# Four chained image layers on one core: gate logits as one product, squares of the next input moved behind the key copies, token transposes moved ahead of a point-wise half

## The chip, the cores and the metric

The kernel runs on one core of one Trainium2 chip. The metric is the device time of one execution in microseconds; lower is better. TensorE is called PE, its weight loads PEld, VectorE DVE, ScalarE ACT, GpSimd POOL and SyncE SP.

## The reference, cut to what matters

Thirty-two images of 256 channels by 28 by 28 pass through four layers, each with a group norm before it and the input added after it.

```python
def reference(x, ...):
    x = x + L0(_gn(x), gate_w, gate_b, expert_w)   # sparsemax gate over 8 experts, mixed 1x1 convolution
    x = x + L1(_gn(x), dw_w, ..., pw_w, ...)       # depthwise 3x3, bn, relu, prune, pointwise 1x1, bn, relu, prune
    x = x + L2(_gn(x), Wqkv, bqkv, Wln, bln)       # linear attention with squared, normalised queries and keys
    x = x + L3(_gn(x), 0)                          # 3x3 box average
    return x

# the gate of L0
pooled = x.mean(axis=(2, 3))
g = sparsemax(pooled @ gate_w.T + gate_b)
w_eff = jnp.einsum('bk,koi->boi', g, expert_w)
out = jnp.einsum('boi,bihw->bohw', w_eff, xs)
```

## The kernel before

**Pipeline.** The 256 channels lie as two halves (j = 0, 1) of 128 partitions. Every engine runs the same function `step(t)` for t from -1 to 36, with t = 8 to 29 in a hardware loop of two steps a turn. In step t seven images are in work, each at another stage: Z = t+1 (input loaded, squares and rounded copy made), A = t (gate and mixed convolution), B = t-1 (depthwise taps), C_ = t-2 (relu and point-wise convolution), D = t-3 (queries and keys), E = t-4 (attention output), F = t-5 (box average). A stage whose image is outside 0 to 31 is left out, so steps 0 to 3 fill the pipeline, steps 4 to 31 are full, and from t = 32 on A is missing (t = 33: A and B; t = 34: A, B and C_). Nothing reorders the work: each engine goes through its `step` as written, and waits on semaphores counted per image.

**PE's order in a step.** `value_out` half 0, `key_norms` (L554), `attention_weights` (L566, L568), `gate_logits` (L509: two products into `small_ps`, one for each half of channels), `value_out` half 1, `attention_out` (L518), `mix_experts` (L648, waits for the gate to be finished), `keys` (L596, L599: seven tiles of 112 tokens in four groups; the fourth group waits for the first two key squares, because it takes their bank), `queries` (L518), `x2_to_tokens` for groups 0 to 2 (L532), `pointwise` (L518), `query_sums` (L618), `x2_to_tokens` group 3, `mixed_conv` (L663), `query_scales` (L630), `keys_x` (L676), `key_sums` (L545), `group_means` (L502). In the steps with C_ but without A, the second half of `pointwise` stands behind `query_sums` and ahead of `x2_to_tokens` group 3.

**DVE's order.** `key_rows` (L968), group norm statistics (L793 to L813), `gate_logits` (L821, L823: the weights of both halves times the pooled input, one instruction on 16 columns), `q_low` (L960), `attention_weights_low` (L981, waits for ACT), `sparsemax` (L831 to L858), `x2_low` (L988), `make_x3` (L922), `h_mask` (L876, waits for ACT), row sums, `h_low`, `mixed_low` (L902), taps (L869), `reciprocal_sums` (L994, waits for the seventh key square), taps, `q_scales` (L1005 to L1011, waits for ACT's L1368), `make_x2` (L890, L894), `make_x1` (L912), `scale_q` (L1019), taps, `kx_low` (L1024).

**ACT's order.** `deviations` (L1161, waits for DVE's L799), `normalise_x2` (L1173), `attention_weights_high` (L1276), relu of h, `x2_high`, `normalise_x3`, `sum_over_h` (L1308), `h_high` (L1317), `scaled_mix` (L1209), `first_tap` (L1292), then the seven squares of keys `square_k` (L1345) with the two squares of the next input `x0_squares` (L1218) behind the second and the third of them, squares of x3, `square_q`, `copy_tokens` (L1246: the transposed tokens scaled into `xT`), fourth powers, `relu_y` 0 (L1335), `sum_over_y` 0 (L1327), `q_norms` (L1368), `relu_y` 1, `sum_over_y` 1, the last token tile, `fourth_powers` (L1268, L1270), `x0_high` (L1227), the squares of x2 and x1, `kx_high` (L1374), `q_high` (L1237), `key_rows` (L1254). Where A is missing, token tiles 0 to 2 are copied before `relu_y` 0, tiles 3 to 5 behind `q_norms`, and tile 6 behind `sum_over_y` 1.

**POOL** scales x1 into `xpad` (L1521); in steps without D and E that waits for the gate product, `gate_step.at(A, 3)`. It also issues the accumulating output DMAs (L1551). **SP** issues the input loads and the output stores.

Of the kernel before, what the change touches and what calls it, by code (L numbers as in the profile page):

```python
# [29 lines left out]
GATE_STEPS = 13  # L30
# [91 lines left out]
def build(nc, x, gate_wT, gate_b, expert_rows, mix_pattern, dw_w, channel_params, pw_wT, w_qk, b_qk, w_vT, w_ln, group_mean, ident, out):  # L122
    with ExitStack() as ctx:
# [88 lines left out]
        gate_in = sb("gate_in", [P, J, EXPERTS])  # L212
        z = sb("z", [P, EXPERTS])
# [233 lines left out]
        def _(pe):  # L447
# [38 lines left out]
            def group_means(Z, A, C_, D, E):  # L486


                if D.active and not A.active:
                    pe.wait_ge(q_root.sem, q_root.at(D))  # L490
                if A.active:
                    pe.wait_ge(gate_step.sem, gate_step.at(A, 4))
                elif A.started:
                    pe.wait_ge(gn_read.sem, gn_read.at(A))
                if Z.active:
                    pe.wait_ge(gn_sums[0].sem, gn_sums[0].at(Z))
                    pe.wait_ge(x0_hi.sem, x0_hi.at(Z))
                for img, layer, made in ((A, 1, x1_ready), (C_, 2, x2_ready), (E, 3, x3_ready)):
                    if img.active:
                        pe.wait_ge(made.sem, made.at(img))  # L500
                        pe.wait_ge(gn_sums[layer].sem, gn_sums[layer].at(img))
                nc.tensor.matmul(small_ps[:, 0:16], gmean[:], gn_in[:].rearrange("p l n -> p (l n)"), start=True,  # L502
                                 stop=True).then_inc(gn_mm.sem, 1)

            def gate_logits(A):
                pe.wait_ge(gn_read.sem, gn_read.at(A))
                pe.wait_ge(gate_step.sem, gate_step.at(A, 3))
                for j in range(J):
                    mm = nc.tensor.matmul(small_ps[:, 0:EXPERTS], ones[:], gate_in[:, j, :], start=(j == 0),  # L509
                                          stop=(j == J - 1))  # L510
                mm.then_inc(gate_mm.sem, 1)
# [168 lines left out]
            def step(t):  # L680
# [29 lines left out]
                if D.active:  # L710
                    query_sums(A, D)
                if C_.active and not A.active:
                    pointwise(C_, range(1, 2))
                if D.active:
                    x2_to_tokens(D, range(3, 4))
# [15 lines left out]
        def _(dve):  # L731
# [84 lines left out]
            def gate_logits(A):  # L816
# [6 lines left out]
                nc.vector.tensor_tensor(gate_in[:], gate_w_sb[:],  # L823
                                        pooled[:, 1, :].unsqueeze(2).to_broadcast([P, J, EXPERTS]),
                                        ALU.mult).then_inc(s.sem, 1)

            def sparsemax(A):
# [4 lines left out]
                dve.wait_ge(s.sem, s.at(A, 4))  # L832
# [3 lines left out]
                dve.wait_ge(s.sem, s.at(A, 5))  # L836
                nc.vector.tensor_tensor(zz[:, 1], zz[:, 0], z[:].unsqueeze(1).to_broadcast([P, EXPERTS, EXPERTS]),
                                        ALU.mult).then_inc(s.sem, 1)
                dve.wait_ge(s.sem, s.at(A, 6))
                nc.vector.tensor_reduce(upper[:, 0:2, :], zz[:], AX.X, ALU.add).then_inc(s.sem, 1)  # L840
                dve.wait_ge(s.sem, s.at(A, 7))
                nc.vector.reciprocal(upper[:, 2, :], upper[:, 0, :]).then_inc(s.sem, 1)
                dve.wait_ge(s.sem, s.at(A, 8))
                nc.vector.scalar_tensor_tensor(upper[:, 3, :], upper[:, 1, :], 1.0, upper[:, 2, :], ALU.subtract,
                                               ALU.mult).then_inc(s.sem, 1)
                dve.wait_ge(s.sem, s.at(A, 9))
                nc.vector.tensor_reduce(tau[:], upper[:, 3, :], AX.X, ALU.max).then_inc(s.sem, 1)
                dve.wait_ge(s.sem, s.at(A, 10))
                nc.vector.scalar_tensor_tensor(gate[:], z[:], tau[:], mix_const[:, 0:EXPERTS], ALU.subtract,
                                               ALU.mult).then_inc(s.sem, 1)  # L850
                dve.wait_ge(s.sem, s.at(A, 11))
                nc.vector.tensor_reduce(gate_own[:], gate[:].rearrange("p (g k) -> p g k", g=PACKED), AX.X,
                                        ALU.add).then_inc(s.sem, 1)
                dve.wait_ge(s.sem, s.at(A, 12))
# [251 lines left out]
        def _(act):  # L1106
# [270 lines left out]
            def step(t):  # L1377
# [42 lines left out]
                for m in range(M):  # L1420
                    if D.active:
                        square_k(D, m)
                    if Z.active and 0 < m <= J:
                        x0_squares(Z, m - 1)
# [20 lines left out]
                if D.active:  # L1445
                    q_norms(A, D)
                    if not A.active:
                        copy_tokens(D, range(3, 6))
# [5 lines left out]
                if D.active:  # L1454
                    copy_tokens(D, range(6, M))
# [22 lines left out]
        def _(pool):  # L1478
# [27 lines left out]
            def normalise_x1(A, B, C_, D, E):  # L1506
# [7 lines left out]
                elif A.active:  # L1514
                    pool.wait_ge(gate_step.sem, gate_step.at(A, 3))
# [117 lines left out]
```

## Time and profile before

| | us |
|---|---|
| median of 3 runs (lowest, highest) | 1503.64 (1500.41, 1505.68) |
| profiled execution, its own time | 1500.17 |
| its span | 1498.5 |
| PE / PEld busy | 1406.2 (94%) / 1238.0 (83%) |
| DVE busy | 1346.3 (90%) |
| ACT busy | 1283.9 (86%) |
| POOL busy | 322.8 (22%) |
| HBM over the span | 85 GB/s |

The span goes from the first to the last instruction; the profiled execution's time is 1.7 us above it. Shares of busy time are means over the filling steps, the full steps and the emptying steps, which have different limits, so the rows below are of one stage each. A timeline row gives start, length, engine, line, operation and the number of instructions merged; an idle time in brackets is that of the engine before the row, with what ended it.

### The profile page before, as it was taken

Reading aid. Unit: us, or ns where it says so; the run is one execution under the profiler, and the core shown is the slowest. Engines: PE = TensorE matmul, PEld = TensorE weight load, DVE = VectorE, ACT = ScalarE, POOL = GpSimd, SP = SyncE. Lnnn points to the kernel's source line nnn. Section 1 sums busy time; section 2 is a strip of 40 time slices with the busy share of each in tenths; the row PEclk is TensorE's granted clock in tenths of the full one; section 3 lists DMA queues with packets and bytes.
Section 4 is the critical chain, followed back from the end, with each engine's and each line's share of the span. In section 5 each row is a group of like instructions: output and inputs, shape, how many; then the busy total and the mean of one; then the engine's idle time right before and its main releaser. Section 6 shows DMA issues by size and latency. Waiting matters only on the chain. (4 is left out here: it accounts for less than half of the span.)

```text
span 1498.5 us, 28620 instructions
## 1 busy us (share of the span) xinstructions
PE 1406.2 (94%) x9538; PEld 1238.0 (83%) x9538; DVE 1346.3 (90%) x2337; ACT 1283.9 (86%) x2624; POOL 322.8 (22%) x298
## 2 busy tenths in 40 slices
PE   3469999999999999999999999999999999999994
PEld 2358898988889898888988888888898888988883
DVE  4889899999999999999999999999999999998647
ACT  5478989989889999988989998898999989888862
POOL 4111122222222221222222122222212222211100
PEclk9679999999999999999999999999999999999997
DMA  4001054353444534344453444345444434444342
GB/s 161 22 22 44 23 108 100 74 108 87 88 89 102 107 70 102 87 94 98 86 107 87 85 94 96 89 86 107 91 80 102 90 86 86 87 88 84 67 66 65
DMA packets 45574, 127.91 MB, mean 85 GB/s; under 512 B 3793, under 2 KB 4817, under 8 KB 45522
## 3 DMA queue, kind: packets, MB, share of 16 engines
q0 software_dynamic: 24480, 72.26, 29.4%
q1 hardware_dynamic: 20946, 54.99, 10.4%
q8 instruction: 29, 0.48, 0.1%
q14 instruction: 23, 0.19, 0.0%
q10 hardware_dynamic: 96, 0.00, 0.0%
HBM read 29.29 MB, written 97.94 MB: 85 GB/s over the span
## 5 line engine op out<-in xcount | busy, mean ns | idle before, releaser
L869 DVE SCALAR_TENSOR_TENSOR h<-xpad,dw_sb,h 128x784 f32<-128x784 f32 x512 | 498.8, 1041 | 0.0
L676 PE MATMUL tile_ps<-k,xT 112*128 112x256 f32 x896 | 200.9, 382 | 3.3 <-ACT xT L1246 3.3
L599 PE MATMUL tile_ps<-wqk,xn_parts 128*112 128x256 f32 x1344 | 191.8, 295 | 0.0
L1551 POOL DMA_DIRECT2D out<-row_sums x90 | 108.8, 1209 | 379.9 <-DMA out<-row_sums 214.7
L676 PEld LDWEIGHTS tile_ps<-k,xT 112*128 112x128 f32 x896 | 168.9, 191 | 25.6 <-issue 3.6
L1538 POOL TENSOR_TENSOR x_parts<-x,x_parts 128x784 fp32r<-128x784 f32 x64 | 109.5, 1729 | 335.5 <-ACT x_parts L1227 335.5
L1167 ACT ACTIVATE junk<-x 128x784 bf16<-128x784 f32 x192 | 163.4, 860 | 9.2 <-DVE x L922 6.4
L599 PEld LDWEIGHTS tile_ps<-wqk,xn_parts 128*112 128x112 f32 x1344 | 170.4, 176 | 0.2
L518 PE MATMUL conv_ps<-xn_parts,w_out 128*128 128x392 f32 x768 | 153.4, 348 | 0.0
L518 PE MATMUL conv_ps<-hq_parts,attn_parts 128*128 128x392 f32 x768 | 145.2, 344 | 3.0 <-DVE attn_parts L981 0.9
L663 PE MATMUL conv_ps<-x_parts,mixed_parts 128*128 128x392 f32 (+1 forms) x768 | 145.3, 345 | 2.1 <-DVE mixed_parts L902 2.1
L518 PE MATMUL conv_ps<-hq_parts,pw_parts 128*128 128x392 f32 x768 | 145.0, 343 | 2.2 <-DVE hq_parts L882 2.2
L518 PEld LDWEIGHTS conv_ps<-hq_parts,attn_parts 128*128 128x128 f32 x768 | 135.0, 188 | 13.0 <-DVE attn_parts L981 13.0
L518 PE MATMUL conv_ps<-xn_parts,wqk 128*128 128x392 f32 x768 | 142.1, 340 | 0.0
L663 PEld LDWEIGHTS conv_ps<-x_parts,mixed_parts 128*128 128x128 f32 x768 | 135.8, 189 | 3.9 <-issue 3.8
L518 PEld LDWEIGHTS conv_ps<-hq_parts,pw_parts 128*128 128x128 f32 x768 | 134.6, 188 | 4.5 <-DVE hq_parts L882 3.9
L518 PEld LDWEIGHTS conv_ps<-xn_parts,wqk 128*128 128x128 f32 x768 | 135.5, 188 | 0.0
L518 PEld LDWEIGHTS conv_ps<-xn_parts,w_out 128*128 128x128 f32 x768 | 134.8, 189 | 0.0
L1521 POOL TENSOR_SCALAR xpad<-x,gn_rs 128x784 f32<-128x784 f32 x64 | 63.6, 1003 | 201.7 <-DVE xn_parts L988 166.5
L1246 ACT ACTIVATE xT<-tile_ps,k_rec 112x256 f32<-112x256 f32 x224 | 89.5, 523 | 0.0
L1345 ACT ACTIVATE k<-tile_ps 112x256 f32<-112x256 f32 x224 | 83.1, 390 | 4.3 <-PE tile_ps L599 4.2
L648 PE MATMUL small_ps<-expert_sb,mix_w 128*32 128x512 f32 x512 | 68.4, 656 | 10.6 <-DVE mix_w L858 10.6
(161 smaller groups left out, 2741.3 us busy)
## 6 DMA issues: line engine op xcount, KB each, us to landing
out<-row_sums POOLq DMA_DIRECT2D x90, 784.0 KB, 7.1
x<-x SPq DMA_DIRECT2D x32, 784.0 KB, 4.3
out<-x SPq DMA_DIRECT2D x30, 784.0 KB, 3.4
expert_sb<-expert_rows SPq DMA_DIRECT2D x8, 256.0 KB, 5.2
out<-x SPq DMA_DIRECT2D x4, 392.0 KB, 2.3
x<-w_qk SPq DMA_DIRECT2D x1, 512.0 KB, 3.6
x<-w_vT SPq DMA_DIRECT2D x1, 256.0 KB, 7.8
x<-w_ln SPq DMA_DIRECT2D x1, 256.0 KB, 7.6
```

The source lines that it names most:

```text
L518: mm = nc.tensor.matmul(conv_ps[:, 2 * j + a, 0:HALF], wt[:, half(j)], act[:, a * HALF:(a + 1) * HALF], start=(first and i == 0), stop=(la ...
L599: mm = nc.tensor.matmul(dst, xn2_parts[:, u, i, m * TOK:(m + 1) * TOK], wqk[:, v, i, C:2 * C], start=False, stop=(i == J - 1 and u == 1))
L648: mm = nc.tensor.matmul(small_ps[s * SUB:(s + 1) * SUB, :], mix_w[:, g, :], expert_sb[:, g, s, :], start=(g == 0), stop=(g == PACKED - 1), ...
L663: mm = nc.tensor.matmul(conv_ps[:, 2 * j + a, 0:width], mixed_parts[:, u, i * C + j * P:i * C + (j + 1) * P], x0_parts[:, v, i, a * HALF:a ...
L676: mm = nc.tensor.matmul(tile_ps[:, KX_BANK, i * C:(i + 1) * C], xT[:, m, half(i)], k2[:, m, :], start=(m == 0), stop=(m == M - 1))
L869: nc.vector.scalar_tensor_tensor(acc, view, scalar, acc, ALU.mult, ALU.add).then_inc(dw_step[j].sem, 1)
L1167: nc.scalar.activation(junk[:, j * HW:(j + 1) * HW], source[:, j, :], ACT.Square, accum_out=gn_in[:, layer, 2 + j:3 + j]).then_inc(gn_sums ...
L1246: nc.scalar.activation(xT[:, m, :], tile_ps[0:TOK, XT_BANK[m // 2], m % 2 * C:(m % 2 + 1) * C], ACT.Identity, scale=k_rec[:, m:m + 1]).the ...
L1345: nc.scalar.activation(k2[:, m, :], tile_ps[0:TOK, K_BANK[m // 2], m % 2 * C:(m % 2 + 1) * C], ACT.Square, accum_out=k_sum[:, m:m + 1]).th ...
L1521: nc.gpsimd.tensor_scalar(xpad[:, j, 1:1 + H, 1:1 + W], x1[:, B.odd, j, :].rearrange("p (h w) -> p h w", w=W), gn_r[:, 1, j:j + 1], gn_s[: ...
L1538: nc.gpsimd.tensor_tensor(x0_parts[:, 1, j, 0:HW], x0[:, Z.odd, j, :], x0_parts[:, 0, j, 0:HW].bitcast(F32), ALU.subtract).then_inc(x0_lo. ...
L1551: pool.dma_start(out_dram[F.times(1)], rows, accum_op=ALU.add).then_inc(rows_added[n].of(F), 16)
```

## The change

Three edits. (1) The gate: DVE multiplies the weights of half 0 by the pooled column into `gate_half`, waits for that, and multiplies half 1 and adds `gate_half` in a second instruction, `gate_sum`; PE forms the logits from `gate_sum` in one product in place of two. All later counts of `gate_step` go up by one; POOL's wait in steps without D and E too. (2) ACT does the seven `square_k` first and the two `x0_squares` behind them. (3) In steps with C_ and D but without A, PE does `x2_to_tokens` group 3 ahead of the second half of `pointwise`, and ACT copies token tiles 3 to 6 in one go behind `q_norms`.

```diff
@@ PE
             def gate_logits(A):
                 pe.wait_ge(gn_read.sem, gn_read.at(A))
-                pe.wait_ge(gate_step.sem, gate_step.at(A, 3))
-                for j in range(J):
-                    mm = nc.tensor.matmul(small_ps[:, 0:EXPERTS], ones[:], gate_in[:, j, :], start=(j == 0),
-                                          stop=(j == J - 1))
-                mm.then_inc(gate_mm.sem, 1)
+                pe.wait_ge(gate_step.sem, gate_step.at(A, 4))
+                nc.tensor.matmul(small_ps[:, 0:EXPERTS], ones[:], gate_sum, start=True, stop=True).then_inc(gate_mm.sem, 1)
...
                 if D.active:
                     query_sums(A, D)
+                if D.active:
+                    x2_to_tokens(D, range(3, 4))
                 if C_.active and not A.active:
                     pointwise(C_, range(1, 2))
-                if D.active:
-                    x2_to_tokens(D, range(3, 4))
@@ DVE
-                nc.vector.tensor_tensor(gate_in[:], gate_w_sb[:],
-                                        pooled[:, 1, :].unsqueeze(2).to_broadcast([P, J, EXPERTS]),
-                                        ALU.mult).then_inc(s.sem, 1)
+                nc.vector.tensor_scalar(gate_half, gate_w_sb[:, 0, :], pooled[:, 1, 0:1], None, ALU.mult).then_inc(s.sem, 1)
+                dve.wait_ge(s.sem, s.at(A, 3))
+                nc.vector.scalar_tensor_tensor(gate_sum, gate_w_sb[:, 1, :], pooled[:, 1, 1:2], gate_half, ALU.mult,
+                                               ALU.add).then_inc(s.sem, 1)
@@ ACT
-                for m in range(M):
-                    if D.active:
+                if D.active:
+                    for m in range(M):
                         square_k(D, m)
-                    if Z.active and 0 < m <= J:
-                        x0_squares(Z, m - 1)
+                if Z.active:
+                    for j in range(J):
+                        x0_squares(Z, j)
...
                 if D.active:
                     q_norms(A, D)
                     if not A.active:
-                        copy_tokens(D, range(3, 6))
+                        copy_tokens(D, range(3, M))
...
                 if D.active:
-                    copy_tokens(D, range(6, M))
+                    if A.active:
+                        copy_tokens(D, range(6, M))
                     fourth_powers(D)
@@ POOL
                 elif A.active:
-                    pool.wait_ge(gate_step.sem, gate_step.at(A, 3))
+                    pool.wait_ge(gate_step.sem, gate_step.at(A, 4))
```

## Rows read from the trace of the kernel before

**Rows 1.** Page: busy time of each engine, share of the span, instructions.

```profile
PE 1406.2 (94%) x9538; PEld 1238.0 (83%) x9538; DVE 1346.3 (90%) x2337; ACT 1283.9 (86%) x2624; POOL 322.8 (22%) x298
```

**Rows 2.** Busy time by stretch (columns named in the first line): steps 4 to 31, and step 33.

```profile
core 0: us, PE busy (x) PEld busy (x) DVE busy (x) ACT busy (x) POOL busy (x), PEclk, DMA share, GB/s
...
130.60:1347.10 1216.50, 1210.71 (x8319) 1070.43 (x8317) 1147.00 (x1988) 1104.97 (x2259) 273.21 (x246) 1.00 0.43 89
...
1387.20:1429.10 41.90, 38.34 (x256) 34.86 (x254) 24.46 (x41) 32.91 (x65) 4.40 (x4) 0.96 0.40 77
```

**Rows 3.** Who waited for whom in steps 4 to 31: total us, times, longest.

```profile
ACT gn_sd L1161 <- DVE gn_var L799: 55.9, 28, 2.0
...
PEld conv_ps L518 <- DVE attn_parts L981: 11.2, 28, 0.5
DVE k_eps L994 <- ACT k L1345: 9.7, 27, 2.8
PEld tile_ps L596 <- ACT k L1345: 9.6, 27, 0.4
...
DVE q_alpha L1005 <- ACT q_norm L1368: 8.9, 27, 0.4
```

**Rows 4.** Timeline of weight loads around the gate product, step 20.

```profile
829.96 0.53 PEld L509 LDWEIGHTS small_ps<-gate_in,ones 128*128 128x128 f32 x4
830.41 0.84 PEld L518 LDWEIGHTS conv_ps<-xn_parts,w_out 128*128 128x128 f32 x5
```

**Rows 5.** Timeline of step 20: ACT's start of the step, then DVE.

```profile
828.55 0.21 ACT L1161 ACTIVATE gn_sd<-gn_var 128x8 f32<-128x8 f32 x1 [2.02 <-DVE gn_var L799]
...
829.32 0.16 DVE L821 TENSOR_TENSOR pooled<-pooled,gn_rs 128x2 f32<-128x2 f32 x1
829.52 0.19 DVE L823 TENSOR_TENSOR gate_in<-gate_w_sb,pooled 128x16 f32<-128x16 f32 x1
...
831.95 0.88 DVE L981 SCALAR_TENSOR_TENSOR attn_parts<-tile_ps,k_inv,attn_parts 128x256 fp32r<-128x256 f32 x2 [0.16 <-ACT attn_parts L1276]
...
839.33 0.17 DVE L876 TENSOR_SCALAR hmask<-h_over 128x2 f32<-128x2 f32 x1 [0.49 <-ACT over L1308]
...
857.21 1.38 DVE L1005 RECIPROCAL q_alpha<-q_norm 128x196 f32<-128x196 f32 x1 [0.32 <-ACT q_norm L1368]
```

**Rows 6.** Timeline: the gate in step 0; ACT in step 2.

```profile
12.63 0.17 DVE L823 TENSOR_TENSOR gate_in<-gate_w_sb,pooled 128x16 f32<-128x16 f32 x1
12.95 0.99 PE L509 MATMUL small_ps<-gate_in,ones 128*128 128x8 f32 x4 [3.42 <-DVE gate_in L823]
...
64.14 2.04 ACT L1292 ACTIVATE h<-xpad,dw_sb 128x784 f32<-128x784 f32 x2 [0.29 <-POOL xpad L1521]
```

**Rows 7.** Timeline: ACT's squares and PE's fourth group of keys, step 20.

```profile
843.98 0.38 ACT L1345 ACTIVATE k<-tile_ps 112x256 f32<-112x256 f32 x1
...
844.34 0.86 ACT L1218 ACTIVATE junk<-x 128x784 bf16<-128x784 f32 x1
...
844.57 0.96 PE L599 MATMUL tile_ps<-wqk,xn_parts 128*112 128x256 f32 x6
```

**Rows 8.** Timeline of PE in step 20, where nothing holds up L676.

```profile
860.70 0.59 PE L630 MATMUL tile_ps<-kx_parts,picks 128*128 128x196 f32 x4
861.12 6.22 PE L676 MATMUL tile_ps<-k,xT 112*128 112x256 f32 x28
```

**Rows 9.** Timeline of PE, end of step 32 to end of step 33.

```profile
1391.58 0.38 PE L554 MATMUL tile_ps<-norm_weight,k_rows 128*128 128x2 f32 x2 [1.70 <-DVE k_rows L968]
...
1418.65 0.69 PE L630 MATMUL tile_ps<-kx_parts,picks 128*128 128x196 f32 x4 [0.19 <-DVE kx_parts L1011]
1421.01 6.28 PE L676 MATMUL tile_ps<-k,xT 112*128 112x256 f32 x28 [1.66 <-ACT xT L1246]
```

**Rows 10.** Timeline of ACT in step 32.

```profile
1378.59 0.45 ACT L1246 ACTIVATE xT<-tile_ps,k_rec 112x256 f32<-112x256 f32 x1
1378.95 0.19 ACT L1268 ACTIVATE k_rec<-k_rec 112x7 f32<-112x7 f32 x1
```

More of the change, by code:

```diff
@@ L29 @@
 PACKED = EXPERTS // STRIPS
-GATE_STEPS = 13
+GATE_STEPS = 14
 XW = HW + 2
@@ L212, in build @@
         gate_in = sb("gate_in", [P, J, EXPERTS])
+        gate_half, gate_sum = gate_in[:, 0, :], gate_in[:, 1, :]
         z = sb("z", [P, EXPERTS])
@@ L491, in group_means @@
                 if A.active:
-                    pe.wait_ge(gate_step.sem, gate_step.at(A, 4))
+                    pe.wait_ge(gate_step.sem, gate_step.at(A, 5))
                 elif A.started:
@@ L831, in sparsemax @@
                 nc.vector.tensor_tensor(z[:], small_ps[:, 0:EXPERTS], gate_b_sb[:], ALU.add).then_inc(s.sem, 1)
-                dve.wait_ge(s.sem, s.at(A, 4))
+                dve.wait_ge(s.sem, s.at(A, 5))
                 nc.vector.tensor_tensor(zz[:, 0], z[:].unsqueeze(1).to_broadcast([P, EXPERTS, EXPERTS]),
@@ L835, in sparsemax @@
                                         ALU.is_ge).then_inc(s.sem, 1)
-                dve.wait_ge(s.sem, s.at(A, 5))
+                dve.wait_ge(s.sem, s.at(A, 6))
                 nc.vector.tensor_tensor(zz[:, 1], zz[:, 0], z[:].unsqueeze(1).to_broadcast([P, EXPERTS, EXPERTS]),
                                         ALU.mult).then_inc(s.sem, 1)
-                dve.wait_ge(s.sem, s.at(A, 6))
+                dve.wait_ge(s.sem, s.at(A, 7))
                 nc.vector.tensor_reduce(upper[:, 0:2, :], zz[:], AX.X, ALU.add).then_inc(s.sem, 1)
-                dve.wait_ge(s.sem, s.at(A, 7))
+                dve.wait_ge(s.sem, s.at(A, 8))
                 nc.vector.reciprocal(upper[:, 2, :], upper[:, 0, :]).then_inc(s.sem, 1)
-                dve.wait_ge(s.sem, s.at(A, 8))
+                dve.wait_ge(s.sem, s.at(A, 9))
                 nc.vector.scalar_tensor_tensor(upper[:, 3, :], upper[:, 1, :], 1.0, upper[:, 2, :], ALU.subtract,
                                                ALU.mult).then_inc(s.sem, 1)
-                dve.wait_ge(s.sem, s.at(A, 9))
+                dve.wait_ge(s.sem, s.at(A, 10))
                 nc.vector.tensor_reduce(tau[:], upper[:, 3, :], AX.X, ALU.max).then_inc(s.sem, 1)
-                dve.wait_ge(s.sem, s.at(A, 10))
+                dve.wait_ge(s.sem, s.at(A, 11))
                 nc.vector.scalar_tensor_tensor(gate[:], z[:], tau[:], mix_const[:, 0:EXPERTS], ALU.subtract,
                                                ALU.mult).then_inc(s.sem, 1)
-                dve.wait_ge(s.sem, s.at(A, 11))
+                dve.wait_ge(s.sem, s.at(A, 12))
                 nc.vector.tensor_reduce(gate_own[:], gate[:].rearrange("p (g k) -> p g k", g=PACKED), AX.X,
                                         ALU.add).then_inc(s.sem, 1)
-                dve.wait_ge(s.sem, s.at(A, 12))
+                dve.wait_ge(s.sem, s.at(A, 13))
                 dve.wait_ge(setup_pool, SETUP_POOL)
```

## The prediction, made before the changed kernel was run

> **What bounds the kernel now.** I read the page first. PE is busy 94%, DVE 90%, ACT 86% [rows 1]; that names no bound, since three engines are nearly full. So I took the busy times by stretch. In steps 4 to 31 PE is busy 1210.71 of 1216.50 us at full clock [rows 2]: 28 steps of 43.45 us, in each of which PE stands still for 5.79 / 28 = 0.21 us. The small rest matters: an engine that is the bound by itself waits for nobody. The view of waits says for whom PE waits: its weight loads wait 9.6 us in all for ACT's key squares at the fourth group of keys, and 11.2 us for DVE's low part of the attention weights [rows 3]. (These are waits of the load queue; the matmuls already in the array hide a good part, which is why the matmuls' idle time is less than their sum.)
>
> Then I followed ACT and DVE round one step. ACT waits for DVE's variance at the start of the step, 55.9 / 28 = 2.0 us; DVE waits for ACT's root of the query sums, 8.9 / 27 = 0.33 us [rows 3]. Between L1161 and L1368 ACT has no wait for PE, and between L1005 and L799 DVE has none, in any full step. So ACT's stretch (L1161 to L1368, 857.21 - 828.55 = 28.7 us in step 20 [rows 5]) and DVE's (L1005 to L799, the other 14.8 us) release each other in a ring, and their sum is the step. **The full steps are set by this ring of ACT and DVE, and PE runs 0.2 us a step ahead of it.** DVE's waits in a full step all lie inside ACT's stretch: 0.16 us at L981 and 0.49 at L876 in step 20 [rows 5], and 9.7 / 27 = 0.36 at L994 and 0.33 at L1005 on the mean [rows 3]. They are the room that DVE has.
>
> Steps 0 to 3 are serial: PE stands idle 3.42 us for the gate in step 0 [rows 6]. In steps 32 and 33 PE waits for the last token tile before L676, 1.66 us each, and between the two 1.70 us before L554 for DVE [rows 9].
>
> **Edit 1, the gate, full steps.** PE drops two of four load and matmul pairs (each product is two). Four take 830.41 - 829.96 = 0.45 us [rows 4], so PE saves 0.225 us a step. DVE gets one more dependent small instruction. Two such follow each other by 829.52 - 829.32 = 0.20 us [rows 5], so DVE pays 0.20 us a step. The sum of halves is then ready at 829.52 + 0.20 + 0.17 = 829.89, and PE's load stood at 829.96 [rows 4, 5]. From ready to matmul takes 0.15 us where PE is waiting (12.80 to 12.95 [rows 6]), so PE is at most 0.1 us late, less than it saves. Behind the added wait on DVE stand the two `q_low` and L981. Of the 0.20 us the wait at L981 takes 0.16 and the wait at L876 the other 0.04, with 0.45 us to spare. As L876 is where DVE next feeds ACT, the ring does not feel it. PE's 0.225 us is in no ring: PE reaches attention_out earlier and waits longer for L981, then for the key squares. Both are worth **0.0 us**. Bounds: -0.225 x 28 = -6.3 us if PE were the bound, +0.20 x 28 = +5.6 us if DVE's room were gone. I take zero because both pools of idle time are there in every full step.
>
> The Trainium skill, VectorE: DVE Perf Modes, section on the TRN2 errata, speaks against this edit: a VectorE instruction on SBUF pays a fixed term of about 150 cycles whatever its size, so halving the columns halves nothing. The trace agrees: 16 columns take 0.19 us and 2 columns 0.16 [rows 5]. By the page's formula for 8 fp32 columns the added instruction is an estimated 0.17 us, 28 of them 4.6 us where the room is gone.
>
> **Edit 1, steps 0 to 3.** Here the four matmuls take 0.99 us [rows 6], against 0.45 from first load to next load in step 20 [rows 4]: PE's clock is at its lower level, and each pair takes about 0.21. Dropping two saves 0.42 us, and DVE adds 0.20: 0.22 us less each in steps 0, 1 and 3, where mix_experts waits for the gate. In step 2 other DVE work stands between, PE's part is hidden, and POOL's `xpad`, for which ACT waits 0.29 us [rows 6], waits for the gate: +0.20. Together 0.20 - 0.66 = **-0.5 us**. Bounds: -0.9 (step 2 gains too) and +0.8 (nothing saved, four times 0.20).
>
> **Edit 2.** The same nine instructions of ACT stand in the same unbroken stretch, so L1368 comes at the same time. A key square takes 844.34 - 843.98 = 0.36 us, a square of the input 0.86 [rows 7]. The seven end 2 x 0.86 = 1.7 us earlier. DVE's wait of 0.36 us at L994 goes; what is late next is L1368, so the same amount appears at L1005. PE waits for the first two squares only, which stay where they were. The seventh square would start at 843.98 + 5 x 0.36 = 845.78; PE, released by the second square, had its fourth group done at 844.57 + 0.96 = 845.53 [rows 7]. Both count from the second square, so ACT gets no new wait, with 0.25 us to spare. The input load, for which the squares wait, has long landed. **0.0 us**; bounds: -0.36 x 28 = -10 us if DVE's wait there were in the ring, +0.25 x 28 = +7 us if PE's fourth group came 0.5 us later than there and ACT waited.
>
> **Edit 3.** It acts in steps 32 and 33 alone; in step 34 C_ is missing, and the order stays. Step 32: PE's two transposes move ahead of the point-wise half (about 0.2 us, and ACT's relu there is not waiting for PE by then). ACT copies the seventh tile, 1378.95 - 1378.59 = 0.36 us [rows 10], ahead of `sum_over_y` 0, so L890, `make_x2`, `scale_q`, eight taps, L1024 and L968, which follow on DVE without a gap, come 0.36 us later. L676 now starts right behind L630. Where nobody waits it starts 0.42 us after it [rows 8], so L676 wins 1.66 us of idle and some 0.3 of overlap, 1.9 in all. But L554 waits for L968, not for that: it starts 0.36 us later, **+0.36 us**, and the 1.9 us turns into wait before it. Step 33 has no taps: L676 is then on the path. It starts at 1418.65 + 0.36 + 0.42 = 1419.43 in place of 1421.01 [rows 8, 9], and what follows moves with it (L545 next waits for the queries that DVE scales, 0.72 us later than before, by my count 0.3 us ahead of need): **-1.6 us** for the end of step 33, the 0.36 included. Bounds for both steps: -2.0 us (nothing on ACT comes later) and +2.1. The latter is the clock: it is granted at 0.96 over step 33 [rows 2], where PE has idled 1.70 us before L554, and that idle becomes about 4 us in one piece. A second such drop would cost at most what the first does, 0.04 x 41.9 = 1.7 us of full-clock work, on top of +0.36.
>
> **Sum.** -0.5 + 0 + 0 - 1.6 = -2.1 us on the profiled execution's 1500.17 (span 1498.5), or 1498.1. That execution lies 3.5 us below the median of the runs, 1503.64, though within their spread of 5.3. Set against the median: **1501.5 us**, 0.14% less.
>
> **Rivals.** *A: PE is the bound after all.* For it: 94% busy, 0.21 us idle a step. Against it: its waits are for ACT and DVE, and these never wait for PE within the ring. It gives -6.3 - 2.1 = 1495.2 us. The Trainium skill, Perfetto Trace Analysis, Identifying the Most-Contended Engine, would judge PE by its weight loads, 83% [rows 1], and so set DVE's 90% first: against A, and for B.
>
> *B: DVE has no room.* Place: between L823 and L876. It decides when the two waits there (0.65 us in step 20) fall below 0.20; the longer DVE stretch then delays ACT's h_high by the added 0.20 in every full step: +5.6 - 2.1 = 1507.1 us, slower than before. Against it: those waits [rows 5].
>
> *C: edit 3 gives nothing.* The idle piece before L554 costs another stretch at the lower clock, or step 33 keeps a wait elsewhere: the tail is 0 to +2.1 us in place of -1.6, so 1503.1 to 1505.2 us.
>
> *D: edit 2 shortens the ring,* since DVE's wait at L994 goes. Against it: L1005 waits for ACT alone. A third of its bound would be 1498 us.
>
> **How the numbers follow.** Forecast 0.68, A 0.09, B 0.07, C 0.12, D 0.04. The range starts from the forecast with the runs' spread (-3.2, +2.0), widened for C above and D below, and leaves out A and B: 1497.0 to 1505.5 us. About 0.3%, 4.5 us, is what a measurement of this kernel can tell from no change, so faster means below 1499.1: A, part of D and the lower edge of the forecast's spread, 0.15. Slower means above 1508.2: B at its upper edge, 0.05. Within 0.3%: 0.80.
>
> **What would show it.** Full steps still 43.4 to 43.5 us; PE idle about 0.4 us in each in place of 0.21; L509 with two loads; DVE's wait at L994 gone and L1005's near 0.6; L876 still waiting for ACT by about 0.3. In step 32 L676 directly behind L630 and a wait near 4 us before L554; in step 33 no wait before L676, and the step about 2 us shorter. Full steps of 43.2 or 43.65 us would make the prediction wrong, towards A or B.

## The result, and the profile after

The changed kernel takes **1511.72 us**, the median of five runs (1508.11 to 1511.92), and the kernel before 1504.6 us in five runs beside it. The ratio is **1.0046, with a 95% interval of 1.0028 to 1.0064**: slower, by about 7 us, where 2.1 us less was forecast and nothing above 1505.5 was in the range. The profiled execution took 1508.11 us, span 1506.4; that of before 1500.17, span 1498.5.

The change did what it says. PE issues 64 products fewer and DVE 32 instructions more than in [rows 1]. The page after, busy time of each engine:

```profile
PE 1405.8 (93%) x9474; PEld 1232.0 (82%) x9474; DVE 1353.5 (90%) x2369; ACT 1289.9 (86%) x2624; POOL 305.2 (20%) x298
```

The shares are those of before. The difference stands in the view by stretch. Columns are the start and end, the length, then busy time and count of PE, PEld, DVE, ACT and POOL, PE's granted clock, the DMA share and GB/s. The three rows are steps 4 to 31, step 32 and step 33:

```profile
130.90:1356.60 1225.70, 1211.69 (x8263) 1065.56 (x8261) 1152.32 (x2016) 1111.10 (x2259) 255.20 (x246) 1.00 0.42 89
1356.60:1394.90 38.30, 36.70 (x255) 33.17 (x253) 30.91 (x48) 34.08 (x67) 6.40 (x6) 1.00 0.41 80
1394.90:1437.10 42.20, 38.02 (x255) 34.67 (x253) 26.68 (x43) 32.73 (x65) 4.40 (x4) 0.96 0.38 72
```

The 28 full steps take 1225.70 us where they took 1216.50 [rows 2]; PE is busy one microsecond more (1211.69 against 1210.71) and stands still 14.0 us in place of 5.8. Step by step, from group means to group means:

| us | start of step 4 | full steps, mean of 28 | step 32 | step 33 | span |
|---|---|---|---|---|---|
| before | 130.63 | 43.445 | 40.16 | 41.82 | 1498.5 |
| after | 130.95 | 43.773 | 38.33 | 42.19 | 1506.4 |

So 28 x 0.328 = +9.2 us in the full steps, +0.3 ahead of them, -1.5 in steps 32 and 33. Together that is +8.0, and the spans differ by 7.9. In this pair of traces the tail did what was forecast; **the loss is 0.33 us in each full step, where the forecast had zero.**

The waits of steps 4 to 31 after (engine and line that waits, on whom: total us, times, longest):

```profile
ACT gn_sd L1160 <- DVE gn_var L797: 60.8, 28, 2.3
DVE q_alpha L1004 <- ACT q_norm L1367: 25.3, 28, 2.2
PEld conv_ps L516 <- DVE attn_parts L980: 19.3, 28, 0.7
DVE hmask L875 <- ACT over L1307: 11.6, 27, 0.5
PE conv_ps L516 <- DVE attn_parts L980: 10.2, 28, 0.4
PEld tile_ps L594 <- ACT k L1344: 9.3, 27, 0.4
```

Against [rows 3]: DVE's wait at the seventh key square is gone, as edit 2 meant. But DVE now waits for the root of the query sums 25.3 / 28 = 0.90 us a step in place of 0.33, which is more than the two waits of before together (0.36 + 0.33), and it waits at `h_mask` as long as ever. DVE did not run out of room at these waits; ACT came later. No row names a new wait of ACT, and this is the puzzle: **ACT's stretch from L1160 to L1367 has grown, though no new wait shows in it.**

To find where, I took the starts of successive rows of the ring that the prediction names and averaged their distances over steps 8 to 29. Three parts of it differ between the kernels; the others agree within 0.02 us:

| us, mean of steps 8 to 29 | `xn` to `attn_parts` (ACT) | first key square to queries (ACT) | queries to the next `over` (ACT) | whole ring |
|---|---|---|---|---|
| before | 1.88 | 5.85 | 6.44 | 43.449 |
| edit 1 alone | 2.04 | 5.86 | 6.45 | 43.640 |
| edit 2 alone | 1.88 | 6.09 | 6.39 | 43.627 |
| after | 2.04 | 6.10 | 6.39 | 43.822 |

There are two places, one for each of the first two edits. (In these 22 steps the kernels differ by 0.37 us; the first and the last full steps differ by less, so that the mean of 28 is 0.33.) The rows behind them come with their experiments.

### The profile page after: what moved, and what is told of

It reads as the page before. It is cut to its first block and busy times, and to the rows that moved or that the text cites. A ratio compares the mean times of both kernels' runs of the same rounds, so it can differ in the third digit from the quotient of the medians.

```text
span 1506.4 us, 28543 instructions
## 1 busy us (share of the span) xinstructions
PE 1405.8 (93%) x9474; PEld 1232.0 (82%) x9474; DVE 1353.5 (90%) x2369; ACT 1289.9 (86%) x2624; POOL 305.2 (20%) x298
## 5 line engine op out<-in xcount | busy, mean ns | idle before, releaser
L1160 ACT ACTIVATE gn_sd<-gn_var 128x8 f32<-128x8 f32 x37 | 7.7, 209 | 89.0 <-DVE gn_var L797 89.0
```

The source lines that it names most:

```text
L1160: nc.scalar.activation(gn_sd[:], gn_var[:], ACT.Sqrt).then_inc(gn_sqrt.sem, 1)
```

## The experiments

Twelve kernels ran. The start of step 4 lies between 130.6 and 133.7 us in the executions profiled, and not in step with the edits: edit 3, which touches no step before 32, had 133.0. It goes with PE's granted clock: over the first 133 us that is 0.83 in the three traces that start step 4 by 131.0 us (before, after, edit 2 alone), and 0.79 to 0.81 in the eleven that start it at 131.8 or later. So spans carry up to 3 us that cannot be put down to an edit, and the kernels are compared by their full steps first, by the ratio of their runs second. The kernel before ran again beside each group of kernels, with medians of 1501.1 to 1504.6 us, so a kernel's time is to be read by its ratio.

### Each edit alone

The first, with edit 1 only: the gate's instructions, its counts, and one product.

```diff
-                nc.vector.tensor_tensor(gate_in[:], gate_w_sb[:],
-                                        pooled[:, 1, :].unsqueeze(2).to_broadcast([P, J, EXPERTS]),
-                                        ALU.mult).then_inc(s.sem, 1)
+                nc.vector.tensor_scalar(gate_half, gate_w_sb[:, 0, :], pooled[:, 1, 0:1], None, ALU.mult).then_inc(s.sem, 1)
+                dve.wait_ge(s.sem, s.at(A, 3))
+                nc.vector.scalar_tensor_tensor(gate_sum, gate_w_sb[:, 1, :], pooled[:, 1, 1:2], gate_half, ALU.mult,
+                                               ALU.add).then_inc(s.sem, 1)
```

> The kernel before with edit 1 alone. Theory T (two handshakes): the gate's second VectorE instruction delays k_inv (L976) by 0.31 us, and ScalarE's first attention-weights instruction (L1276), which had 0.2 us to spare, starts 0.17 us later behind its xn instruction: full steps 43.6 us, 28 x 0.17 = +4 to +5 us. Rival B (VectorE alone has no room, edit 1 explains everything): full steps 43.8 us, +8 to +10 us. Rival U (neither edit alone costs, only together): within 1 us of before.

Measured: 1506.52 us, ratio 1.0036 (1.0023 to 1.0049), full steps 43.603 us, +0.16. Step 20 of the kernel before, ACT's `xn` and `attn_parts`, and DVE from the gate on:

```profile
829.23 1.98 ACT L1173 ACTIVATE xn<-x,gn_rs 128x784 f32<-128x784 f32 x2 [0.26 <-DVE gn_rs L813]
831.11 0.81 ACT L1276 ACTIVATE attn_parts<-tile_ps,k_inv 128x256 fp32r<-128x256 f32 x2
...
829.63 0.97 DVE L960 TENSOR_TENSOR hq_parts<-q,hq_parts 128x784 fp32r<-128x784 f32 x1
...
830.72 0.17 DVE L976 RECIPROCAL k_inv<-k_inv 128x2 f32<-128x2 f32 x1
```

The same of the kernel after:

```profile
834.73 1.98 ACT L1172 ACTIVATE xn<-x,gn_rs 128x784 f32<-128x784 f32 x2 [0.26 <-DVE gn_rs L811]
836.77 0.84 ACT L1275 ACTIVATE attn_parts<-tile_ps,k_inv 128x256 fp32r<-128x256 f32 x2
...
835.02 0.23 DVE L821 TENSOR_SCALAR gate_in<-gate_w_sb,pooled 128x8 f32<-128x8 f32 x1
835.28 0.23 DVE L823 SCALAR_TENSOR_TENSOR gate_in<-gate_w_sb,pooled,gate_in 128x8 f32<-128x8 f32 x1
835.44 0.96 DVE L959 TENSOR_TENSOR hq_parts<-q,hq_parts 128x784 fp32r<-128x784 f32 x1
836.32 0.15 DVE L973 TENSOR_SCALAR k_inv<-k_norm 128x2 f32<-128x2 f32 x1
836.51 0.17 DVE L975 RECIPROCAL k_inv<-k_inv 128x2 f32<-128x2 f32 x1
```

ACT's `attn_parts` (the high part of the attention weights) reads `k_inv`, the reciprocal of the key norms. DVE makes that behind the gate and `q_low` 0. Before, it was complete at 830.72 + 0.17 = 830.89, and ACT came for it at 831.11: 0.22 us to spare. In the kernel after it is complete at 836.68, and ACT starts at 836.77, 2.04 us behind the start of `xn` and no longer 1.88. The wait is there, but ACT loses only 0.16 us by it, and the view puts no idle time beside so short a gap. In the kernel with edit 1 alone `k_inv` is complete at 836.06 + 0.17 = 836.23 and ACT starts at 836.33:

```profile
834.28 1.98 ACT L1172 ACTIVATE xn<-x,gn_rs 128x784 f32<-128x784 f32 x2 [0.26 <-DVE gn_rs L811]
836.33 0.84 ACT L1275 ACTIVATE attn_parts<-tile_ps,k_inv 128x256 fp32r<-128x256 f32 x2
...
836.06 0.17 DVE L975 RECIPROCAL k_inv<-k_inv 128x2 f32<-128x2 f32 x1
```

The next, with edit 2 only:

```diff
-                for m in range(M):
-                    if D.active:
+                if D.active:
+                    for m in range(M):
                         square_k(D, m)
-                    if Z.active and 0 < m <= J:
-                        x0_squares(Z, m - 1)
+                if Z.active:
+                    for j in range(J):
+                        x0_squares(Z, j)
                 if E.active:
                     junk_free((Z, gn_sums[0]))
                     sum_squares(3, E, x3_of(E), x3_ready)
```

> The kernel before with edit 2 alone. Theory T: the squares of x3, which wait for the squares of x0 because both write the scratch tile junk, now follow them directly, and ScalarE stands still for about 0.25 us between the two: full steps 43.6 to 43.7 us, +5 to +7 us. Rival B: no change, ScalarE's work is the same, within 1 us of before. Rival U: within 1 us of before.

Measured: 1505.32 us, ratio 1.0030 (1.0019 to 1.0042), full steps 43.609 us, +0.16. The last three lines of that diff, which the change leaves alone, are the cause. The squares of x0 and those of x3 write their unused output into the same scratch tile, `junk`, and `junk_free` makes the x3 squares wait until those of x0 are done. Step 20 with edit 2 alone, ACT (L1218 squares x0, L1167 squares x3):

```profile
849.71 0.90 ACT L1218 ACTIVATE junk<-x 128x784 bf16<-128x784 f32 x1
850.46 0.24 ACT L1218 ACTIVATION_READ_ACCUMULATOR junk<-x 128x1 f32 x1
...
850.81 0.86 ACT L1167 ACTIVATE junk<-x 128x784 bf16<-128x784 f32 x1
...
851.67 0.84 ACT L1167 ACTIVATE junk<-x 128x784 bf16<-128x784 f32 x1
```

From the second x0 square to the first x3 square it is 1.10 us, where two squares that don't wait for each other follow at 0.86: the wait on the instruction directly ahead costs 0.24 us. It was always there, but four key squares stood between the two, so that it was met long before it was asked for. The same gap can be read in the kernel before at a place that no edit touched: the last square of x2 and the first of x1, where `junk_free` stands between the two:

```profile
863.70 0.84 ACT L1167 ACTIVATE junk<-x 128x784 bf16<-128x784 f32 x1
864.45 0.19 ACT L1167 ACTIVATION_READ_ACCUMULATOR junk<-x 128x1 f32 x1
...
864.75 0.86 ACT L1167 ACTIVATE junk<-x 128x784 bf16<-128x784 f32 x1
```

They start 1.05 us apart, while the two x2 squares ahead of them are 0.84 apart. Of the 0.24 us the ring gets 0.05 back between the queries and the next `over` (table above); what ends that part earlier I haven't found.

The third, with edit 3 only (group 3 of the transposes ahead of the second point-wise half in steps with C_ and D but without A, and `copy_tokens(D, range(3, M))` at once).

> The kernel before with edit 3 alone. All theories: full steps stay 43.45 us, steps 32 and 33 together 1.5 us shorter, with the wait before the key norms (L554) near 4 us and none before L676. -1.5 us in the span; the clock rival of the prediction would give 0 to +2 us.

Measured: 1500.77 us, ratio 0.9995 (0.9986 to 1.0003). Full steps are 43.462 us, as before. Step 32 takes 38.29 us and step 33 42.19, together 80.48 in place of 81.98: -1.5 us. But step 34, which the edit leaves alone, takes 38.09 us in this trace in place of 36.73, at a lower granted clock (0.91 against 0.95, the number behind POOL's; first this trace, then the kernel before):

```profile
1430.42:1468.51 38.09, 35.25 (x232) 31.30 (x230) 16.78 (x28) 21.87 (x47) 4.40 (x4) 0.91 0.44 75
1429.07:1465.80 36.73, 33.89 (x231) 30.20 (x229) 16.80 (x28) 21.84 (x47) 4.40 (x4) 0.95 0.35 56
```

Over steps 32 to 34 almost nothing is left of the gain (118.58 us against 118.72), and the interval of the ratio holds both -1.5 us and nothing.

The parts add up: 0.158 + 0.164 = 0.322 us a full step for edits 1 and 2, and 0.328 measured for both.

### Each cause mended in the kernel after

Edit 2's place first. The first x3 square gets a scratch tile of its own, so it waits for nobody.

```diff
+        junk3 = sb("junk3", [P, HW], BF16)
...
-                    junk_free((Z, gn_sums[0]))
-                    sum_squares(3, E, x3_of(E), x3_ready)
+                    if (E - 1).active:
+                        act.wait_ge(gn_sums[3].sem, gn_sums[3].at(E - 1))
+                    for j, spare in enumerate((junk3[:], junk[:, 0:HW])):
+                        act.wait_ge(x3_ready.sem, x3_ready.at(E, j + 1))
+                        if j:
+                            junk_free((Z, gn_sums[0]))
+                        nc.scalar.activation(spare, x3_of(E)[:, j, :], ACT.Square,
+                                             accum_out=gn_in[:, 3, 2 + j:3 + j]).then_inc(gn_sums[3].sem, 1)
```

> The changed kernel, but the first half of x3's squares goes to a scratch tile of its own and the second half to the part that the first x0 square has long left, so that nothing waits for the instruction right ahead of it. Theory T: the 0.25 us stand between the x0 squares and the x3 squares goes, the delay of L1276 stays: full steps 43.6 us, 5 to 7 us less than the changed kernel. Rival B: no change against the changed kernel, full steps 43.8 us. Rival U: back to the time of before, since one of the two is gone.

Measured: 1506.08 us, ratio to before 1.0036 (1.0022 to 1.0049), full steps 43.592, so 0.18 us less than after. The four squares now stand 0.84 us apart (L1435 is the new line):

```profile
851.11 0.91 ACT L1218 ACTIVATE junk<-x 128x784 bf16<-128x784 f32 x1
...
851.95 0.90 ACT L1218 ACTIVATE junk<-x 128x784 bf16<-128x784 f32 x1
...
852.79 0.90 ACT L1435 ACTIVATE junk<-x 128x784 bf16<-128x784 f32 x1
...
853.63 0.90 ACT L1435 ACTIVATE junk<-x 128x784 bf16<-128x784 f32 x1
```

Then edit 1's place: DVE makes `k_inv` ahead of the gate.

```diff
+                if E.active:
+                    key_norms(E)
                 if A.active:
                     gate_logits(A)
                 if E.active:
                     q_low(E, 0)
-                    key_norms(E)
                     q_low(E, 1)
```

> The changed kernel with VectorE's key_norms (L973, L975) put ahead of the gate, so that k_inv no longer stands behind the gate's second instruction; VectorE does the same instructions as in the changed kernel. Theory T (place): ScalarE's L1275 follows xn without a wait, edit 1's 0.16 us a step go, the 0.16 us of edit 2 stay: full steps 43.61 us, 4 to 5 us less than the changed kernel. Rival B (VectorE has no room): the amount of work is the same, so no change: 43.77 us.

Measured: 1505.86 us, ratio 1.0030 (1.0019 to 1.0041), full steps 43.646, 0.13 us less than after. `xn` to `attn_parts` is 1.88 us again, though DVE is as busy as in the kernel after: what mattered was where the gate stood, not how much of it there was. The 0.04 us by which this full step lies above that of edit 2 alone (43.609) I haven't traced.

Both at once:

> The changed kernel with both mends: the scratch tile split and VectorE's key_norms ahead of the gate. Theory T: both added handshakes are gone, full steps 43.45 to 43.50 us as before, and the 1.5 us of edit 3 remain: between -2 and +1 us against before. If a third cost hides in the change, it stays at +3 us or more.

Measured: 1501.89 us, ratio 0.9992 (0.9982 to 1.0001), full steps 43.455, as before (43.445). **The two places are the whole of the 0.33 us.** What is left is the change as the prediction saw it in the full steps, untouched, and no gain that a ratio can show. In this trace steps 32 and 33 take 81.48 us, only 0.5 less than before; why comes with edit 3 below.

### A double dose

If the wait for `k_inv` is the cause of edit 1's cost, a further instruction ahead of it must be paid in full in every step. On edit 1 alone, a third dependent instruction of the same size behind the two (the counts that follow go up by one):

```diff
+                dve.wait_ge(s.sem, s.at(A, 4))
+                nc.vector.tensor_scalar(gate_half, gate_w_sb[:, 0, :], pooled[:, 1, 0:1], None, ALU.mult).then_inc(s.sem, 1)
```

> Edit 1 alone, with one more dependent small VectorE instruction behind gate_sum that nobody needs (PE and GpSimd wait for gate_sum as before). Theory T: the spare 0.15 us ahead of L1276 are used up by edit 1, so the next instruction is paid in full: 0.20 to 0.26 us a step more than edit 1 alone, full steps 43.80 to 43.86 us, +6 to +7 us on edit 1 alone. A theory in which edit 1 costs through its TensorE side or through code placement gives no more than edit 1 alone, 43.60 us.

Measured: 1515.07 us, ratio 1.0090 (1.0077 to 1.0104), full steps 43.941: +0.34 us over edit 1 alone, all of it between `xn` and `attn_parts` (2.38 us). That is more than expected. Averaged over steps 8 to 29 the third instruction costs 0.25 us; the other 0.07 lie ahead of the gate, where `pooled` (L819) starts up to 0.36 us later in some of the steps. What holds it up there isn't known. Now the wait is long enough for the view of waits to name it:

```profile
ACT attn_parts L1277 <- DVE k_inv L977: 9.4, 26, 0.7
```

### Is the ring the bound, and what is PE's saving worth?

A rival to the ring is that PE bounds the step. The kernel before, with the first two key squares moved ahead of ACT's first tap, so that PE's fourth group of keys never waits:

```diff
+                if D.active:
+                    for m in range(2):
+                        square_k(D, m)
                 if B.active and t.number not in (1, 2):
                     for j in range(J):
                         first_tap(B, j)
```

(and the later loop starts at m = 2).

> The kernel before with one move: ScalarE does the first two key squares ahead of first_tap, so that TensorE's fourth group of keys no longer waits. Ring theory: TensorE's wait there (0.17 us in even steps) goes, but the ring is untouched: full steps stay 43.45 us, within 1 us of before. If TensorE were the bound: full steps 43.3 us, -3 to -4 us.

Measured: 1500.0 us, ratio 0.9980 (0.9970 to 0.9989). The full steps are 43.454, unchanged, and the wait at L596 is gone. PE idles 0.15 us a step in place of 0.20: the 0.06 at L518 are as before, and 0.10 at L554 are new. The gain in the traces lies in steps 32 to 34, 115.86 us in place of 118.72, at a granted clock of 0.97 in both; what makes it isn't known. A wait of PE taken away gives nothing while the ring is as long as it was.

Next the ring itself. The squares of x0 leave ACT's stretch between L1161 and L1368 for the time behind it, in which ACT waits for DVE anyway (55.9 us in [rows 3]). On the kernel after with `key_norms` first:

```diff
+                late_x0 = t.number is None or t.number >= 3
...
-                if Z.active:
+                if Z.active and not late_x0:
                     for j in range(J):
                         x0_squares(Z, j)
                 if E.active:
-                    junk_free((Z, gn_sums[0]))
                     sum_squares(3, E, x3_of(E), x3_ready)
...
                     x0_high(Z)
+                    if late_x0:
+                        junk_free((E, gn_sums[3]))
+                        for j in range(J):
+                            x0_squares(Z, j)
...
-                    junk_free((E, gn_sums[3]), (Z, gn_sums[0]))
+                    junk_free((Z, gn_sums[0]), (E, gn_sums[3]))
```

> The changed kernel with key_norms ahead of the gate and, from step 3 on, the two squares of x0 behind x0_high, that is out of ScalarE's stretch of the ring and into the stretch in which it waits for VectorE. Ring theory: the ring gets 1.7 us shorter and PE becomes the bound: 43.45 - 0.21 of idle - 0.22 of the dropped product = 43.0 us a full step, -12 us in the loop and -1.5 in the tail against before, near 1490 us. If ScalarE's total work bounded the step, no gain; if its late squares delay its key rows (L1253), a wait of up to 0.4 us appears at VectorE's L967.

Measured: 1497.64 us, ratio 0.9974 (0.9964 to 0.9985), full steps 43.352. The part from the first key square to the queries fell by 1.7 us (5.85 to 4.18), but the next one rose by 1.2 (6.44 to 7.65), and DVE's part from `scale_q` to `key_rows` by 0.35, at the end of which DVE's `key_rows` now starts as ACT's ends (870.33 and 870.30 us). So only a tenth of a us came through, against the 0.45 expected. The larger part of the miss is a new wait in the middle of ACT's stretch; step 21:

```profile
892.79 0.92 ACT L1353 ACTIVATE q<-conv_ps,bq_col 128x784 f32<-128x784 f32 x1 [1.10 <-PE conv_ps L516]
```

ACT is at the second half of the queries before PE has made it, and PE is late because its fourth group of keys waited for ACT's second key square: a longer ring through all three engines. The remedy is the move of the last experiment, put on top:

> The kernel with late x0 squares, key_norms first and the new gate, and now also the first two key squares ahead of first_tap. With late x0 squares the ring ran through TensorE (ScalarE to the second key square, TensorE's fourth group and the queries, ScalarE's L1353 with 1.1 us of wait). If that is so, freeing the fourth group makes TensorE the bound: 43.15 to 43.2 us a full step in place of 43.36, another -4 to -6 us, 1491 to 1493 us. If not, no change.

Measured: **1486.94 us (1485.44 to 1487.89), ratio 0.9890 (0.9876 to 0.9904), full steps 42.98.** It beats both kernels, and by more than expected (43.15 to 43.2). Its steps 4 to 31 by stretch:

```profile
133.70:1337.20 1203.50, 1202.11 (x8263) 1066.53 (x8261) 1155.83 (x2016) 1111.79 (x2260) 255.36 (x246) 1.00 0.43 90
```

PE idles 1.39 us in 28 steps, 0.05 a step. That does not make its work as long as the step: the same 8263 products count 1211.69 us busy in the kernel after and 1202.11 here, so PE's busy time holds some waiting too, and how near PE is to being the bound stays open.

Does edit 1's product saved count for something there? The same two kernels with the gate of before (two products, one instruction of DVE):

> The same, but with the gate of before: one VectorE instruction, two products. If PE is the bound in both, this one is 0.22 us a full step slower, 43.23 us, and 5 to 6 us slower in all: the gain that edit 1 can give where PE is the bound. If the ring is still the bound, the two are equal.

Measured: 1497.31 us, ratio 0.9972 (0.9963 to 0.9982), full steps 43.383, against 43.352 with the new gate.

> The same with the gate of before (one VectorE instruction, two products). Where TensorE is the bound, its dropped product (0.22 us a step) is worth what its wait for the later gate sum leaves of it: 0.05 to 0.2 us a step slower than the kernel with the new gate, 1.5 to 5 us. Equal, if that wait eats it all.

Measured: 1487.91 us, ratio 0.9893 (0.9878 to 0.9907), full steps 42.979, against 42.980. Even with PE busy nearly throughout the saved product gives nothing. With the new gate PE's load of the logits' product waits for DVE (steps 4 to 31 of the kernel with the new gate):

```profile
PEld small_ps L509 <- DVE gate_in L823: 4.6, 22, 0.3
```

That is 0.2 us in each of 22 steps, about what the two pairs save (0.225 us). The matmuls say the same. Averaged over steps 8 to 29, from the start of PE's last matmul ahead of the gate's to the first behind them it is 0.53 us with the new gate and 0.48 with the old one: PE gets past the gate no sooner. Both kernels have `key_norms` first, though, which puts the gate later. Where it stands ahead of them, PE does get past sooner, in 0.36 us in the kernel after and 0.48 in the one before. Whether those 0.12 us would count in the fastest kernel was not tried.

## Why the prediction was wrong

**The bound: right.** The ring of ACT and DVE sets the full step. A delay in it is paid in full (the double dose), PE's wait alone is worth nothing (the early key squares), and ACT's stretch 1.7 us shorter gives 0.47 us a step once PE's late keys are out of the way, where without that it gives 0.1. The ring is the bound, then, but the next limit, in part the longer ring through PE, lies only 0.1 us behind it. Rival A falls for the kernel before.

**Edit 1, full steps: wrong, by the step on where DVE next feeds ACT, with a term of the sum that was too small besides.** The size first: "DVE pays 0.20 us a step", taken from two `TENSOR_TENSOR` instructions [rows 5]. The pair that came has a column as scalar operand. It takes 0.23 us each, starts 0.26 apart, and `q_low` follows L823's start by 0.16 where it was 829.63 - 829.52 = 0.11: 0.26 + 0.05 = 0.31 us. The trace of before had an instruction of that form, in `sparsemax`, with `tau` as the column, and it takes 0.23 us there too:

```profile
834.41 0.23 DVE L849 SCALAR_TENSOR_TENSOR gate<-z,tau,mix_const 128x8 f32<-128x8 f32 x1
```

The Trainium skill, VectorE: DVE Perf Modes, on the TRN2 errata, was rightly called to say that halving the columns halves nothing (0.19 us for 16 columns, 0.23 for the new forms on 8); its formula, an estimated 0.17 us, is below the row.

The step that failed is the other: "As L876 is where DVE next feeds ACT, the ring does not feel it." DVE feeds ACT earlier. `k_inv` stands between the two `q_low` in the same queue, ACT's `attn_parts` reads it, and the room there was 831.11 - 830.89 = 0.22 us less some 0.1 for the hand-over, so about 0.13. Of 0.31 us of delay that leaves 0.18; 0.16 was measured. (Averaged over steps 8 to 29 instead of read in one step: room 0.238 us, hand-over 0.095, `k_inv` 0.303 later, which leaves 0.160.) I had looked for DVE's waits for ACT as "the room that DVE has". They say how early DVE comes to them, not how late it may be for its readers. The prediction's check of L981 was of no use for the same reason: L981 waits for ACT, which waits for `k_inv`.

Rival B had the right kind of loss, on the wrong wait: it asked whether the waits between L823 and L876 fell short of 0.20. The one at `h_mask` is still 11.6 / 27 = 0.43 us, and the price came without it.

**Edit 1, steps 0 to 3: wrong for step 0, the rest open.** -0.5 us was forecast, -0.22 of it in step 0. There the products do take 0.57 us in place of 0.99, as the term had it:

```profile
12.59 0.23 DVE L821 TENSOR_SCALAR gate_in<-gate_w_sb,pooled 128x8 f32<-128x8 f32 x1
13.23 0.57 PE L509 MATMUL small_ps<-gate_in,ones 128*128 128x8 f32 x2 [3.75 <-DVE gate_in L823]
16.54 1.24 DVE L857 SCALAR_TENSOR_TENSOR mix_w<-gate_own,zeros,mix_const 128x64 f32<-128x64 f32 x1
```

But from the start of the gate to that of `mix_w`, for which `mix_experts` waits, it is 16.54 - 12.59 = 3.95 us. In the kernel before the gate starts at 12.63 [rows 6], and `mix_w` as long after it, 3.95:

```profile
16.58 1.24 DVE L858 SCALAR_TENSOR_TENSOR mix_w<-gate_own,zeros,mix_const 128x64 f32<-128x64 f32 x1
```

So nothing of it is left there. That PE was at its lower clock in step 0 no row shows either: the view of windows gives 1.00 from 12 to 14 us, and only the longer products (0.99 against 0.45 us) speak for it. For steps 1 to 3 the starts of step 4 scatter by 3 us with the granted clock, so that the pair's 0.3 us says nothing.

**Edit 2: wrong.** "The same nine instructions of ACT stand in the same unbroken stretch" holds for the instructions and not for their waits: `junk_free` ahead of the x3 squares, a line that the diff shows only as its surroundings, was met by distance and is now met by waiting, 0.24 us, of which 0.16 to 0.18 reaches the step. Forecast right in it: DVE's wait at the seventh key square is gone and stands at L1004 instead. It was put near 0.6 us and is 0.90: the 0.36 + 0.33 = 0.69 of before, and 0.24 - 0.05 = 0.19 by which ACT comes later behind `h_mask`, make 0.88. ACT has no wait for PE at the queries, as forecast. Rival D falls: with DVE's wait at the seventh key square gone the full step of edit 2 alone is longer, and with the scratch tile mended too (both mends) it is 43.455 us, no shorter than before.

**Edit 3: the working right, what it is worth open.** The kernel after, PE's scales and the 28 products at the end of step 32, the key norms behind them, and the end of step 33:

```profile
1386.38 0.69 PE L628 MATMUL tile_ps<-kx_parts,picks 128*128 128x196 f32 x4 [0.24 <-DVE kx_parts L1010]
1386.91 6.23 PE L674 MATMUL tile_ps<-k,xT 112*128 112x256 f32 x28
...
1401.50 0.38 PE L552 MATMUL tile_ps<-norm_weight,k_rows 128*128 128x2 f32 x2 [3.94 <-DVE k_rows L967]
...
1428.58 0.69 PE L628 MATMUL tile_ps<-kx_parts,picks 128*128 128x196 f32 x4 [0.24 <-DVE kx_parts L1010]
1429.10 3.21 PE L674 MATMUL tile_ps<-k,xT 112*128 112x256 f32 x14
```

The 28 products follow the scales without idle time, where they waited 1.66 us [rows 9], and what they won stands as a wait of 3.94 us ahead of the key norms (forecast: about 4). Steps 32 and 33 together changed by 80.52 - 81.98 = -1.46 us, forecast -1.6. How it falls on the two depends on where a step is cut: group means stand between L676 and L554, so the 1.9 us that L676 was to win count to step 32 and are given back in step 33. Cut like that, the forecast says -1.9 and +0.3; measured are -1.83 and +0.37. The clock over step 33 is 0.96 in this trace, as before, and so the longer idle piece cost nothing more in it.

Rival C (another stretch at the lower clock) does not fall by that. Of the nine traces that have edit 3, four (the own scratch tile, both mends, the late x0 squares, and the fastest kernel with the old gate) show step 33 at a granted clock of 0.92, and it takes 43.1 to 43.6 us there; here that of both mends:

```profile
1387.85:1431.10 43.25, 39.08 (x255) 35.75 (x254) 26.65 (x43) 32.89 (x65) 4.62 (x4) 0.92 0.38 73
```

That is 0.9 to 1.4 us more than the 42.2 at 0.96, most of what edit 3 gains, and a fifth trace, edit 3 alone, loses as much in step 34. Traces without the edit scatter too: the clock of step 33 is 1.00 in that of edit 2 alone, that of edit 1 alone has 0.96 in step 32 and in step 33, which take 83.0 us together, and that of the double dose has 0.91 in step 34. So at equal clock edit 3 gives 1.5 us, its runs alone give a ratio of 0.9986 to 1.0003, and whether it makes the lower stretches more frequent stays open.

**Sum.** -0.5 + 0 + 0 - 1.6 was forecast. Measured in the traces of before and after (the first and the last term carry the scatter of the clock): +0.3, +0.16 x 28 = +4.4, +0.16 x 28 = +4.6, -1.5, together 7.8 of 7.9 us. The sign was wrong by two waits that neither the view of waits nor a bracket in the timeline could show, since each had been met before its reader asked. The prediction named the reading that would refute it ("Full steps of 43.2 or 43.65 us"); they came at 43.77.

## What to carry to other kernels

An edit that delays an engine inside a ring has to be checked against every reader of what that engine makes, each with its room: when the operand is complete, against when the reader starts. The view of waits lists only the waits that were not met; the room of the one that mattered here was 0.13 us. Before taking an instruction's cost from a neighbour, look for one of the same form, operands included; the trace of before had one. When instructions of an in-order queue change places, list the waits that stand ahead of their neighbours too, for a wait that distance used to meet costs time when it follows its writer directly. And in a ring, shorten the ring first (moving work to where its engine waits anyway), then look for the next ring, and only last save work on the engine that is busiest. A gain of a few us in the stages where PE idles is to be compared at equal granted clock, for one trace of each kernel can show it or hide it.

## What the runs showed of the hardware

- Two VectorE instructions on 128x8 with a column as scalar operand, the second waiting for the first, start 0.26 us apart and are busy 0.23 us each; two on tensors alone (128x2, then 128x16) start 0.20 apart. Both take longer on their 8 columns than the one on 16 columns (0.19). The same holds in the kernel before for `gate` (L849), 128x8 with a column as scalar operand: 0.23 us.
- A ScalarE square of 128x784 with an accumulated sum that waits for the square directly ahead of it starts 1.05 to 1.10 us after it, and 0.84 to 0.86 us after it if it doesn't wait.
- From the end of DVE's reciprocal to the start of the ACT instruction that waits for it takes 0.09 to 0.10 us (836.68 to 836.77, 836.23 to 836.33). A gap of that kind has no bracket in the timeline, so a chain that is bound by it looks like unbroken work.
- PE's granted clock in the emptying steps differs between executions of nearly the same code. Of the nine traces with edit 3, five have 0.96 over step 33, which takes 42.2 us, and four 0.92, where it takes 43.1 to 43.6.
- Over the filling steps it differs as well: 0.83 over the first 133 us where step 4 starts at 130.6 to 131.0 us, 0.79 to 0.81 where it starts at 131.8 to 133.7.
